# Four attention units at once on TensorE: scores and values of a whole block in one group of matmuls

## What is computed

```
x = L0(x, ctx)      # channel attention: softmax(q k) v + x, one head of 256 x 256 per batch
x = L1(x, ctx)      # layernorm, self attention of 16 heads of width 16, + x;
                    # layernorm, cross attention to ctx, + x; layernorm, MLP with gelu, + x
x = L2(ctx, x)      # 16 heads, x asks, [ctx, x] answers (256 keys), + x; rmsnorm, MLP with gelu, + x
x = L3(x, ctx)      # two cross attentions with 16 heads of width 128, then an MLP

# in L1 and L2, for each head:
s = q @ k.T * scale            # 128 x 128 (L1) or 128 x 256 (L2)
p = softmax(masked(s))         # along the keys
o = p @ v                      # 128 x 16
```

## The kernel before

| slot | scores of | work ahead of the transposes | work between the two transposes |
|---|---|---|---|
| 0 | self 0 | lat_v | ctx_k, rms |
| 1 | self 1 | - | - |
| 2 | self 2 | ctx_v | mlp2_up0 to up3 |
| 3 | self 3 | cross_o | - |
| 4 | lat 0 | mlp2_down0 | - |
| 5 | lat 1 | ln3 | mlp2_down1 |
| 6 | lat 2 | chan_q | chan_k |
| 7 | lat 3 | self_o | chan_v |
| 8 | chan 0 | cross_k | mlp1_up0 to up3 |
| 9 | chan 1 | ln2 | - |
| 10 | lat 4 | cross_q | - |
| 11 | lat 5 | mlp1_down0 | - |
| 12 | lat 6 | mlp1_down1 | - |
| 13 | lat 7 | cross_v | - |
| 14 | cross 0 | ln1 | lat |
| 15 | cross 1 | self_q | lat_q |
| 16 | cross 2 | self_k | lat_k |
| 17 | cross 3 | self_v | lat_o |

## Time and profile before

### The profile page before, as it was taken

The page is one execution under the profiler, slowest core; times in us unless marked ns, Lnnn a source line. Parts: engine busy times, 40 slices in busy tenths (PEclk is TensorE's granted clock), DMA queues, the critical chain, the costliest instruction groups (busy, mean ns, idle before and its releaser), DMA issues.

```text
span 2292.3 us, 43483 instructions
## 1 busy us (share of the span) xinstructions
PE 2094.7 (91%) x14880; PEld 1799.8 (79%) x14880; DVE 1292.5 (56%) x4117; ACT 1168.0 (51%) x3854; POOL 679.7 (30%) x618
## 2 busy tenths in 40 slices
PE   5788999999999998986899999999799999999798
PEld 3566777777777776764799999998699999999687
DVE  3658675758576765333555555555555555555654
ACT  3556665756656565543444444444444444444432
POOL 2223333333333343221322222223222222123343
PEclk8999999999999999998899999999999999999989
DMA  6000000000000000000100000000000000000100
GB/s 240 3 1 11 1 11 1 10 1 11 1 6 6 1 4 2 3 1 24 36 24 14 23 23 23 18 23 22 8 24 23 18 23 14 23 23 14 37 14 23
DMA packets 23658, 45.19 MB, mean 20 GB/s; under 512 B 2400, under 2 KB 10080, under 8 KB 22624
## 3 DMA queue, kind: packets, MB, share of 16 engines
q1 hardware_dynamic: 21440, 32.62, 4.6%
q10 hardware_dynamic: 1440, 8.72, 1.0%
q0 software_dynamic: 640, 2.10, 0.3%
HBM read 41.33 MB, written 2.10 MB: 19 GB/s over the span
## 4 chain that ended last, share of the span: by engine, by line
issue 39%; POOL 8%; PE 3%; DVE 1%; POOLq 0%; DMA 0%; ACT 0%; SPq 0%; DVEq 0%; ACTq 0%
POOL probs L1220 2%; POOL w_qk L1196 2%; PE general L1730 2%; PE general L1574 1%; POOL w_o L1196 1%; POOL w_v L1196 1%; DVE oT L1556 1%; POOL X L1236 1%; POOL hT L1211 1%; POOL vrow L1200 1%; DMA raw_vrows<-vrows_dram 0%; PE general L1585 0%; DVE oT L1559 0%; DVE ctxT L1550 0%; POOLq L1195 0%
## 5 line engine op out<-in xcount | busy, mean ns | idle before, releaser
L431 POOL TENSOR_TENSOR probs<-probs,rsums 128x512 f32<-128x512 f32 (+1 forms) x288 | 283.4, 992 | 643.0 <-DVE rsums L632 641.9
L471 ACT ACTIVATE probs<-negated,negmax 128x128 f32<-128x128 f32 (+1 forms) x768 | 326.2, 429 | 66.3 <-DVE negmax L623 65.7
L1220 POOL TENSOR_TENSOR probs<-probs,rsums 128x512 f32<-128x512 f32 x128 | 133.2, 1041 | 764.3 <-DVE rsums L1418 764.3
L915 PE MATMUL pT_psum<-ident,probs 128*128 128x128 f32 x1088 | 177.3, 285 | 63.8 <-DVE probsT L638 39.1
L1327 ACT COPY probsT<-pT_psum 128x512 f32<-128x512 f32 x128 | 75.0, 586 | 288.3 <-PE pT_psum L1671 288.3
L915 PEld LDWEIGHTS pT_psum<-ident,probs 128*128 128x128 f32 x1088 | 128.2, 145 | 113.6 <-issue 84.9
L1574 PE MATMUL general<-hT,w_qk 128*128 128x512 f32 x768 | 207.0, 405 | 4.0 <-POOL hT L1211 4.0
L1574 PE MATMUL general<-w_o,oT 128*128 128x256 f32 x1536 | 194.8, 281 | 16.4 <-DVE oT L1425 16.4
L1574 PEld LDWEIGHTS general<-w_o,oT 128*128 128x128 f32 x1536 | 186.1, 188 | 24.6 <-DVE oT L1425 18.1
L1574 PE MATMUL general<-ctxT,w_qk 128*128 128x512 f32 x768 | 200.4, 397 | 0.0
L1319 ACT ACTIVATE probs<-scores,negmax 128x128 f32<-128x128 f32 x512 | 180.5, 370 | 29.8 <-DVE negmax L1410 29.7
(11 more groups left out here) (173 smaller groups left out, 4165.5 us busy)
## 6 DMA issues: line engine op xcount, KB each, us to landing
raw_qk<-w_qk_dram SPq DMA_DIRECT2D x34, 256.0 KB, 2.7
raw_v<-w_v_dram SPq DMA_DIRECT2D x17, 256.0 KB, 2.6
raw_vrows<-vrows_dram SPq DMA_DIRECT2D x17, 256.0 KB, 3.2
weights_a<-weights_a_dram ACTq DMA_DIRECT2D x2, 2048.0 KB, 18.2
raw_o<-w_o_dram SPq DMA_DIRECT2D x16, 256.0 KB, 2.6
weights_a<-weights_a_dram ACTq DMA_DIRECT2D x3, 1024.0 KB, 10.2
X<-x_dram SPq DMA_DIRECT2D x8, 256.0 KB, 7.4
ctx_in<-ctx_dram SPq DMA_DIRECT2D x8, 256.0 KB, 3.9
```

Source lines behind the costliest of these rows:

```text
L431: nc.gpsimd.tensor_tensor(pr, pr, rsums[:, n % 4, 0:segs].unsqueeze(2).broadcast_to([P, segs, width(kind) // segs]), ALU.mult).then_inc(s[ ...
L471: last = nc.scalar.activation(probs[:, n % PROBS, i * wide:(i + 1) * wide], src[:, i * wide:(i + 1) * wide], ACT.Exp, scale=1.0 if kind == ...
L915: last = nc.tensor.transpose(pT_psum[:, j * P:(j + 1) * P], probs[:, n % PROBS, j * P:(j + 1) * P], ident[:, :])
L1220: nc.gpsimd.tensor_tensor(pr, pr, rsums[:, t % 2, :].unsqueeze(2).broadcast_to([P, NB, P]), ALU.mult).then_inc(s["probs_ready"], 1)
```

## The change

In self, cross and lat the scores of all four units of a block are computed in the slot of the block's first pair, and the values of all four in the slot where the second pair's values stood. The four units' matmuls follow one another on the four bands, where they had followed one another on two. The semaphores rise by 4 at the end of a group. The scores wait for the fourth bank's reading (`n + 3`) where they waited for the second's (`n + 1`). The values stand ahead of the slot's first transposes, where they stood between the two. In `chan` only the place of the values changes. DVE's first wait of a unit is for all four units of the block; nothing else changes on DVE, ACT, POOL or SP.

```
-                    dve.wait_ge(s["scores_ready"], n + 1 if kind == "chan" else n // 2 * 2 + 2)
+                    dve.wait_ge(s["scores_ready"], n + 1 if kind == "chan" else (n // 4 + 1) * 4)
...
                     n = index(kind, g, 2 * p)
-                    wait_bank_read(n + 1)
...
                     if kind == "chan":
+                        wait_bank_read(n + 1)
...
-                    segs = segments(kind)
-                    for j in range(segs):
-                        for e in range(2):
+                    wait_bank_read(n + 3)
+                    for j in range(segments(kind)):
+                        for e in range(4):
                             out = score_bank(n + e)
-                            band = slice(32 * (r + e), 32 * (r + e) + 32)
+                            band = slice(32 * e, 32 * e + 32)
...
-                            if j == segs - 1:
-                                last.then_inc(s["scores_ready"], 1)
+                    last.then_inc(s["scores_ready"], 4)
...
-                    for e in range(2):
+                    units = BLOCK_UNITS[kind]
+                    u0 = 2 * p + 2 - units
+                    n = index(kind, g, u0)
+                    c, b, _ = unit_parts(kind, u0)
+                    for e in range(units - 2, units):
                         wait_pT_copied(pe, n + e)
-                    i = block_of(kind, g, 2 * p)
+                    wait_block_read(pe, block_of(kind, g, u0) - 1)
...
                     for j in range(4):
-                        for e in range(2):
-                            band = slice(32 * (r + e), 32 * (r + e) + 32)
+                        for e in range(4):
+                            band = slice(32 * e, 32 * e + 32)
...
-                            if j == 3:
-                                last.then_inc(s["pv_done"], 1)
+                    last.then_inc(s["pv_done"], 4)
...
-                    if pair:
+                    if pair and 2 * pair[2] % BLOCK_UNITS[pair[0]] == 0:
                         scores_of(*pair)
                     for name, g in work[:1]:
                         other_work(name, g)
+                    weighed = pair_at(slot - WEIGH_AFTER)
+                    if weighed and (2 * weighed[2] + 2) % BLOCK_UNITS[weighed[0]] == 0:
+                        weigh_values(*weighed)
                     turned = pair_at(slot - TRANSPOSE_AFTER)
                     if turned:
                         kind, g, p = turned
                         transpose_probs(kind, g, 2 * p)
-                    weighed = pair_at(slot - WEIGH_AFTER)
-                    if weighed:
-                        weigh_values(*weighed)
```

More of the change, by code:

```diff
@@ L890, in scores_of @@
                             wait_copied(pe, name, g)
-                    c, b, r = unit_parts(kind, 2 * p)
+                    c, b, _ = unit_parts(kind, 2 * p)
                     if kind == "chan":
+                        wait_bank_read(n + 1)
                         for e in range(2):
@@ L918, in weigh_values @@
                 def weigh_values(kind, g, p):
-                    n = index(kind, g, 2 * p)
-                    c, b, r = unit_parts(kind, 2 * p)
-                    for e in range(2):
+                    units = BLOCK_UNITS[kind]
[3 more added lines that the diff above has]
+                    for e in range(units - 2, units):
                         wait_pT_copied(pe, n + e)
-                    i = block_of(kind, g, 2 * p)
+                    wait_block_read(pe, block_of(kind, g, u0) - 1)
                     out = o_psum
-                    if 2 * p % BLOCK_UNITS[kind] == 0:
-                        wait_block_read(pe, i - 1)
-                    if p == 0:
+                    if u0 == 0:
                         for name in {"lat": ("lat_v", "ctx_v")}.get(kind, (kind + "_v",)):
@@ L938, in weigh_values @@
                     for j in range(4):
-                        for e in range(2):
-                            band = slice(32 * (r + e), 32 * (r + e) + 32)
+                        for e in range(4):
+                            band = slice(32 * e, 32 * e + 32)
                             pT = probsT[:, (n + e) % 4, j * P:(j + 1) * P]
-                            head = c * HPC + 2 * (r + e) + (j // 2 if kind == "lat" else j % 2)
+                            head = c * HPC + 2 * e + (j // 2 if kind == "lat" else j % 2)
                             columns = slice(32 * head, 32 * head + 32)
```

## The result

The kernel after takes 2320.61 us (median of 2 runs, 2319.33 to 2321.89) against 2299.55; the ratio of the two is put at 1.0088, with a 95% interval of 1.0063 to 1.0112. It is slower by 21 us where I forecast 7 us less. The profiled execution took 2321.89 us, its span is 2320.2.

What follows compares the result with a forecast made beforehand. PE was taken to nearly bound the middle (94% busy). Six periods at -0.6 give -4, the drain -4, the filling nothing: 2294.0 becomes 2286 profiled, 2292 on the median's scale. Forecast 2280 to 2305; range 2260 to 2325 us.

Steps and rivals of the forecast that it cites:

- Four abreast: Scores and values of four units run together on four bands, 1.09 and 1.02 us a group, removing 16.4 us a period.
- the rival by which a group of four units costs two groups: Groups cost 2.1 and 2.0 us, only lat's scores gain; net +5 us a period, 2335 us; chance 0.08.
- The waits of a period: PE's waits in a middle period: ACT's copies 9.8, DVE's 5.1, inputs 4.5, score banks 1.8; 21.2 us, 14.7 new.
- The period: One middle period: 1.7 us less at full clock, 1.1 lost to the clock, net -0.6; six periods -4 us.
- 0.7 more per period: Middle: 0.7 more slow-clock stretches in each period, allowed at 1.1 us.
- My rival of the falling clock: Clock falls at each of a period's three waits of 2 us or more: 17 us more, 2309 us; chance 0.15.
- my own sign for it: Changed profile: a granted clock below 0.96 in the middle would show that the clock case holds.
- The filling: First 197 us: PE already idles 56 us, DVE and ACT set the pace; no change, within 10 us either way.
- The drain: Eight slots of lat lose their scores, 1.06 us each; half of that, 4 us, is gained.

Runs made afterwards that it cites:

- scores_fillers: Kernel after with only the scores in fours, values in pairs between the transposes, plus dummy matmuls in 95 of its own waits: 2242.08 us.
- before_fillers: Kernel before plus dummy matmuls in 74 of its own waits, 76 us in all: 2270.57 us.
- pairs_ahead: Kernel after without any group of four: scores and values in pairs, the values still ahead of the first transposes: 2352.77 us.
- fillers_early: Kernel after plus dummy matmuls only in the 40 waits of the filling, before slot 48: 2298.02 us.
- fill_pairs: Kernel after with blocks before slot 48 done as before, in pairs with the values between the two transposes: 2307.26 us.
- fillers_tiny: Kernel after plus one dummy matmul of only 4 columns at each of 134 waits: 2319.62 us.
- scores_only: Kernel after with only the scores in fours; values stay in pairs between the transposes: 2270.10 us.
- values_only: Kernel after with only the values in fours, ahead of the first transposes; scores stay in pairs: 2344.43 us.

## Why the prediction was wrong

- **Four abreast: right.** 32 passes take what 16 took, and the rival by which a group of four units costs two groups is excluded. The Trainium skill (TensorE: Matmul & The Clock Gate, "Part 2: What happens when you issue a matmul") puts the sequencer's work at about 62 ns for each matmul where hardware decoding is off. That does not bind here: 1.17 us for 32 passes is 37 ns a pass.
- **The waits of a period: right.** ACT's copies 9.2 (9.8 laid out), DVE's 5.6 with the values' waits (5.1), inputs 3.6 (4.5), score banks 1.5 (1.8). PE's 103.08 busy us contain the clock's loss of at most 4.9 us (0.04 x 123), so 98 or a little more at full clock, where I had 99.
- **The period: right by two errors.** I wrote -1.7 for the work and the waits and +1.1 for the clock. With the clock held the middle is 14.5 us shorter in 4.5 periods, 3.2 each, so in these two executions the gain was about twice as large. The clock's part was too small as well: 17.9 us in after against 4.9 in before, 2.9 more per period where I allowed 1.1. The term "0.7 more per period" is the mis-sized one: the stretches at the low level came in each period and not sometimes (the clock of both of after's periods is 0.96). My rival of the falling clock had 24 us more than before over six periods (30 less 6); 2.9 a period are 17 over six. It was the right mechanism, and my own sign for it came, a middle below 0.96 (0.95 over the 604 us); but it had no word on the filling.
- **The filling: the step that failed.** "DVE's and ACT's work of each slot sets the pace; I take nothing, within 10 either way." With the clock held, "nothing" is right: 3.0 us less, of which 2.6 are the first load. But it is a balance: the fours of scores alone shorten the filling by 8.8 us (scores_fillers against before_fillers; 5.9 without the first load), so DVE and ACT don't set its pace by themselves, and the values' half takes 5.8 back. What I passed over is that the earlier trace rows already had a clock of 0.90 there: the waits multiplied and the clock fell to 0.81 up to 211 us. My reading is that at half speed PE's work no longer fitted into the time that DVE and ACT left it. The result is 21.8 us up to the first cut (16.5 and 17.5 in the two other executions of this filling), where I had nothing; 2.2 of them are the first load (15.0 against 12.8 us).
- **The drain: wrong in sign.** I took -4; with the clock held it is -3.5, without that it came out at +3.2 between the last two cuts, again at a lower clock (0.91 against 0.96).
- **The sign.** -16.8 us with the clock held, +21 with the clock as it falls. And the sum was over the whole change where its halves are -28 and +46: my own list had 14.9 of 21.2 us of waits on copies, which belong mostly to the values, and 1.8 on score banks, which belong to the scores, and I never priced the scores alone.

The half-speed time itself is a bad price. The clock of after up to the last cut (0.83 over 295.1, 0.96 over 548.9, 0.91 over 230.1) means about 2 x (0.17 x 295.1 + 0.04 x 548.9 + 0.09 x 230.1) = 186 us at the low level, and holding the clock gave back 28.0 + 17.9 + 14.3 = 60. The Trainium skill (TensorE: Matmul & The Clock Gate, "HAM oscillation — how this bites in real kernels") prices a throttled stretch at half its length. By that rule my estimate would be 93 here. The measured share is about a third: as I read it, part of each stretch is waiting that the clock doesn't lengthen.

What brings the clock of the filling down is known in part. It does not follow the waits for ACT's copies alone. Those of pairs_ahead up to its first cut are as many and as long in sum as after's 26 and 22.1 us:

```profile
PE pT_psum L940 <- ACT probsT L503: 22.8, 27, 3.2
```

and its clock there is 0.90, after's 0.83. Without dummy matmuls of full size, the kernels with values in pairs in the filling have 0.90 to 0.93 there, those with values in fours 0.81 to 0.85, wherever the values stand. So it goes with the groups of four values; why, is open. Open is also why the drain of kernels with the same groups there took 230.1 us at clock 0.91 (after) and 233.9 to 234.0 at 0.88 and 0.89 (fillers_early, fill_pairs, fillers_tiny).

## What to carry to other kernels

Work that stands between two dependent steps of an engine is cover, and shortening it or moving it away can cost what it hid: price each half of an edit by itself, since here one gained 28 us and the other lost 46. Where TensorE is not the bound, its waits are still not free: look at the granted clock of that stretch first, and if it is already under full speed, don't put added waits at nothing. A copy of the kernel with dummy matmuls in its waits tells in one run what the clock costs, and if nothing better covers the waits it can stay: scores in fours with values in pairs and dummy matmuls is 2.35% faster than before.

## What the runs showed of the hardware

- Waits in sum do not settle the clock. pairs_ahead waits 10.8 us in a period (126.9 less 116.14 busy) and runs the middle at 1.00, before waits 6.5 and runs it at 0.99, after 20 at 0.96. The longest wait of the period is 2.4 us in the first two and 3.1 in after.
- A wait for score banks of 6.4 us in the filling, the longest after the first load, brought no lateness by itself: scores_only has it and ends the filling 0.3 us later than before, at clock 0.91, while values_only, without it, ends it 26.0 us later at 0.81. Whether it eats part of what the fours of scores gain there is not taken apart.
- The dummy matmuls, about 97 us of work that nobody needs (440 of 0.22 us), make the kernel 28 us faster (scores_fillers against scores_only).
